# An AdaLN block on one core: batch 4's second FFN half behind the last projection, two of the last products and the sixth batch's shift on GpSimd

## The chip, the cores and the metric

The kernel runs on one NeuronCore of a Trainium2 chip. The metric is the device time in microseconds of one execution; three runs of the kernel before gave 286.42, 286.42 and 287.06 us, median 286.42. TensorE, VectorE, ScalarE and GpSimd run side by side, each through its own queue in order; SyncE issues all DMA. They meet only at semaphores.

## What is computed

Eight batches (B = 8) of 512 tokens by 256 channels, all fp32. Each goes through a layer norm modulated by rows made from a condition, an attention with 16 heads in which token i sees itself and i - 2^k (ten offsets, 0 to 256), a projection with gate and residual, a second modulated layer norm, a quantisation to fp6 in blocks of 32 (then scaled back), one 256x256 linear layer (called FFN), and gate and residual again.

```python
h = _layernorm(x) * (1 + ca) + sa
x = x + ga * attention(h, Wq, bq, Wk, bk, Wv, bv, Wo, bo)
h = _layernorm(x) * (1 + cb) + sb
xq, xs = _mx_quantize(h); wq, ws = _mx_quantize(weight)
x = x + gb * ((xq * xs) @ (wq * ws).T + bias)
```

The scores outside the ten offsets are 0, not minus infinity, so the softmax counts them: `out` is a sum of ten products of weights and shifted rows of v, plus a mean of v.

## The kernel before

Tokens lie on 128 partitions in four tiles (`NT` = 4), so a batch is a 128x1024 tile; a half is two tiles. The order of the work on each engine is written out by hand in five blocks (`block.sync`, `gpsimd`, `tensor`, `scalar`, `vector`), each a list of small functions; every function waits on counted semaphores and then issues. `LAST` is 7. Batches 0 to 5 are in a pipeline loop; the tail, after some 210 us, is written out call by call, and the change lies wholly there. In it:

- **Batch 7's products** (`pv_product(LAST, n)`, L1851). VectorE multiplies softmax weights (in the PSUM tile `ps45`) by the rows of v for ten offsets, n = 0 to 9. TensorE transposes each into `ps01` and sums it there (`last_product`, L919: eight matmuls for a product, six for n = 8, four for n = 9). ScalarE then seeds `ps45` with the residual (`seed_projection`, L1334), takes the sum out of `ps01` (`evacuate_last_attention`, L1352), and TensorE projects it (`project(LAST)`, L988).
- **Batch 6's second norm.** `project(LAST-1)`, then on ScalarE `take_x1`, `squares_after` (L1238, ending in the variance, L1242), on GpSimd `rstd_after` (L666, L668), on ScalarE `norm_after` (L1174); GpSimd scales by a modulation row (`scale_sixth`, L683) and VectorE adds the other (`shift_sixth`, L1766). VectorE then does `block_maxima`, `quantise`, `dequantise`.
- **Batch 7's second norm** is done in halves: VectorE's `last_variance` (L1595 to L1605) for half 0, GpSimd's `rstd_after(LAST, 0)`, ScalarE's `norm_last(0)` (L1174 with `v_shift`).
- **The gated FFN weights.** GpSimd multiplies `wT` by the row `row_gb` (`gate_ffn`, L639). There is one `row_gb` buffer: SyncE's `load_row_gb(b)` (L433) waits until gate b-1 is done, and gate b waits for the load.
- **Batch 4's FFN** (LAST-3) is in halves, both in `ps67`: `ffn(LAST-3, 1)` stands between the summed attention of batch 6 and `project(LAST-1)` on TensorE. `take_result` (L1407) copies a finished half out on ScalarE and counts `s_outb` ("out_ready").
- **Batch 5's FFN** (LAST-2) is in `ps23`, behind `xd_transposes(LAST-2)` (L1009), a copy of the transposes by ScalarE (`evacuate_xd`, L1365) and three filler matmuls (`keep_busy`, L752).

## Time and profile before

| | |
|---|---|
| median of 3 runs | 286.42 us |
| span of the profiled execution | 285.0 us |
| VectorE busy | 258.8 us (91%) |
| TensorE matmul busy | 255.6 us (90%) |
| ScalarE busy | 212.5 us (75%) |
| GpSimd busy | 210.5 us (74%) |
| granted TensorE clock, mean | 1.000 |

The span is from the first to the last instruction of one execution; the time of a run is 1.4 us longer than it. Busy shares are over the whole span; what counts for this change is which engine waits for which in the last 45 us, and that is in the timeline.

### The profile page before, as it was taken

The numbers are of one execution on the slowest core, as the hardware profiler recorded it, in microseconds if no ns is written. First come the engines' busy times: TensorE is split into PE (matmuls) and PEld (weight loads), VectorE is DVE, ScalarE is ACT, GpSimd is POOL, SyncE is SP. The second block draws the span as 40 slices with busy tenths as digits, with TensorE's granted clock in tenths as the row PEclk, the third lists the DMA queues.
The fourth block names the chain that finished last, engine by engine and source line by source line (L and its number), as shares of the span: only waits on it lengthen the run. The fifth ranks groups of instructions, "written<-read, shape, count | busy, mean of one in ns | idle before, by whom it ended". The sixth has DMA issues, their size and how long they took to land.

```text
span 285.0 us, 4442 instructions
## 1 busy us (share of the span) xinstructions
PE 255.6 (90%) x1368; PEld 158.8 (56%) x1368; DVE 258.8 (91%) x326; ACT 212.5 (75%) x577; POOL 210.5 (74%) x152
## 2 busy tenths in 40 slices
PE   6999997697978795989999999999999988997885
PEld 1653554175526561666556646664567646794663
DVE  3699799969995999999999999999999999999970
ACT  2386987975697779879898989887776937575752
POOL 7101439895879999999999999999999699845100
PEclk9999999999999999999999999999999999999999
DMA  7743977694784239724993389347943965730005
GB/s 225 193 181 81 340 248 232 230 338 133 240 273 148 73 125 350 251 72 131 295 336 127 129 263 286 135 113 222 333 147 94 279 198 178 230 103 11 0 26 199
DMA packets 54399, 53.91 MB, mean 189 GB/s; under 512 B 4100, under 2 KB 52824, under 8 KB 54376
## 3 DMA queue, kind: packets, MB, share of 16 engines
q1 hardware_dynamic: 54376, 53.63, 60.1%
q8 instruction: 11, 0.18, 0.3%
q14 instruction: 12, 0.10, 0.1%
HBM read 44.90 MB, written 8.72 MB: 188 GB/s over the span
## 4 chain that ended last, share of the span: by engine, by line
DVE 39%; POOL 19%; PE 18%; issue 11%; ACT 11%; DVEq 0%; POOLq 0%; ACTq 0%
POOL pv_buf L677 14%; DVE prod L1721 9%; DVE pv_buf L1851 9%; DVE prod L1851 4%; DVE prod L1710 4%; PE ps L988 3%; PE ps L1067 3%; PE ps L826 2%; ACT dump L1197 2%; PE ps L853 2%; ACT dump L1238 1%; DVE ps L1825 1%; PE ps L837 1%; DVE ps L1827 1%; POOL rstd L658 1%
## 5 line engine op out<-in xcount | busy, mean ns | idle before, releaser
L677 POOL TENSOR_TENSOR pv_buf<-pv_buf 128x1024 f32<-128x1024 f32 (+2 forms) x60 | 132.5, 2209 | 15.0 <-DVE pv_buf L1851 9.8
L1721 DVE TENSOR_TENSOR prod<-ps,kT 128x1024 f32<-128x1024 f32 (+4 forms) x70 | 75.1, 1110 | 0.0
L1851 DVE TENSOR_TENSOR pv_buf<-v_shift,ps 128x1024 f32<-128x1024 f32 x49 | 59.1, 1212 | 0.0
L937 PE MATMUL ps<-prod,sel_sum 128*32 128x512 f32 x256 | 30.8, 598 | 8.5 <-DVE prod L1721 7.8
L853 PE MATMUL ps<-wT,h_cen 128*128 128x256 f32 x128 | 29.9, 379 | 0.0
L826 PE MATMUL ps<-hT,wT 128*128 128x512 f32 x64 | 29.7, 596 | 0.0
L837 PE MATMUL ps<-hT,wT 128*128 128x512 f32 x64 | 29.3, 599 | 0.0
L988 PE MATMUL ps<-wo_g,w_raw 128*128 128x256 f32 x112 | 27.9, 392 | 0.0
L853 PEld LDWEIGHTS ps<-wT,h_cen 128*128 128x128 f32 x128 | 23.9, 190 | 6.4 <-issue 3.8
L988 PEld LDWEIGHTS ps<-wo_g,w_raw 128*128 128x128 f32 x112 | 20.1, 189 | 5.4 <-issue 3.2
L937 PEld LDWEIGHTS ps<-prod,sel_sum 128*32 128x32 f32 x256 | 6.7, 109 | 28.0 <-issue 13.8
L1067 PE MATMUL ps<-wf_g,w_raw 128*128 128x256 f32 x80 | 19.7, 391 | 0.0
L1851 DVE TENSOR_TENSOR pv_buf<-v_base,ps 128x1024 f32<-128x1024 f32 (+2 forms) x21 | 19.4, 950 | 0.2
L1291 ACT ACTIVATE kT<-ps,bias_cols 128x512 f32<-128x512 f32 x16 | 10.9, 686 | 11.6 <-PE ps L826 11.6
L649 POOL TENSOR_TENSOR rstd<-var,minus_half 128x4 f32<-128x4 f32 x4 | 4.1, 1016 | 20.1 <-ACT var L1201 19.3
L1174 ACT ACTIVATE x_norm<-x_in,shift,rstd 128x256 f32<-128x256 f32 x28 | 14.5, 594 | 5.6 <-POOL shift L651 3.2
L837 PEld LDWEIGHTS ps<-hT,wT 128*128 128x128 f32 x64 | 11.7, 190 | 12.4 <-issue 12.4
L826 PEld LDWEIGHTS ps<-hT,wT 128*128 128x128 f32 x64 | 11.6, 190 | 10.5 <-issue 9.0
L1067 PEld LDWEIGHTS ps<-wf_g,w_raw 128*128 128x128 f32 x80 | 14.5, 189 | 3.6 <-issue 2.0
L1174 ACT ACTIVATE x_norm<-x,shift,rstd 128x256 f32<-128x256 f32 x28 | 14.5, 592 | 1.4 <-POOL shift L668 1.4
L380 POOL TENSOR_TENSOR h<-x_norm,rows_mod 128x1024 f32<-128x1024 f32 x6 | 14.2, 2362 | 0.5
L375 POOL TENSOR_TENSOR x_norm<-x_norm,rows_mod 128x1024 f32<-128x1024 f32 x6 | 14.2, 2364 | 0.3 <-ACT x_norm L1174 0.2
(212 smaller groups left out, 550.3 us busy)
## 6 DMA issues: line engine op xcount, KB each, us to landing
v_shift<-v_rows SPq DMA_DIRECT2D x56, 512.0 KB, 5.7
x_in<-in_L_attn_x SPq DMA_DIRECT2D x8, 512.0 KB, 4.4
v_rows<-v_base SPq DMA_DIRECT2D x8, 512.0 KB, 4.1
x_res<-in_L_attn_x SPq DMA_DIRECT2D x8, 512.0 KB, 6.5
out_x<-outb SPq DMA_DIRECT2D x5, 512.0 KB, 5.8
rows_mod<-mod_rows SPq DMA_DIRECT2D x7, 256.0 KB, 3.4
x<-in_L_wmod SPq DMA_DIRECT2D x1, 1024.0 KB, 7.9
row_ga<-mod_rows SPq DMA_DIRECT2D x8, 128.0 KB, 4.9
```

The lines of the kernel that those rows point to most:

```text
L375: ops.tensor_tensor(normed[:, t, :], normed[:, t, :], rows[:, 0:1, :].broadcast_to([P, n, D]), ALU.mult).then_inc(scaled, 1)
L380: ops.tensor_tensor(dst[:, t, :], normed[:, t, :], rows[:, 1:2, :].broadcast_to([P, n, D]), ALU.add).then_inc(done, 1)
L677: nc.gpsimd.tensor_tensor(dst, dst, ring(b, n)[:, t:NT, :], ALU.add).then_inc(s_add, 1)
L826: mm = nc.tensor.matmul(ps23[:, j, :], wT[:, 1, k, P * j:P * j + P], hT[:, k, :], start=(k == 1), stop=(k == 0))
L837: mm = nc.tensor.matmul(ps01[:, j, :], wT[:, 0, k, P * j:P * j + P], hT[:, k, :], start=False, stop=(k == NC - 1), skip_group_check=True)
L853: mm = nc.tensor.matmul(ps23[:, k2, col:col + D], h_cen[:, k, P * t:P * t + P], wT[:, 2, k, :], start=(t % 2 == 0 and k == 0), stop=(t % 2 ...
L937: mm = nc.tensor.matmul(ps23[32 * g:32 * g + 32, 1, :], sel_sum[:, which, c, :], prod[:, n, c, :], start=(c == 0 and which == 0), stop=(c ...
L988: mm = nc.tensor.matmul(ps[:, k2, col:col + D], attnT[:, k, P * t:P * t + P], wo_by[b][:, k, :], start=False, stop=(t % 2 == 1 and k == NC ...
L1067: mm = nc.tensor.matmul(ps[:, half_, col:col + D], xdT_by[b][:, k, P * t:P * t + P], wf_by[b][:, k, :], start=False, stop=(t % 2 == 1 and ...
L1174: ins = nc.scalar.activation(dst[:, t, :], src[:, t, :], ACT.Identity, scale=rstd[:, t:t + 1], bias=shift[:, t:t + 1])
L1721: nc.vector.tensor_tensor(prod[:, n, :, o:L], ps01[:, :, o:L], kT[:, b % 2, :, 0:L - o], ALU.mult).then_inc(s_prod, 1)
L1851: nc.vector.tensor_tensor(dst[:, t:NT, :].rearrange("p t (h e) -> p t h e", e=DH), v_n.rearrange("p t (h e) -> p t h e", e=DH), weights, A ...
```

## The change

GpSimd takes over three pieces: batch 7's products 8 and 9 (new `far_product`, with their weights normalised first into the SBUF tile `w_far`), and the shift of batch 6, so that it does the whole `modulate`. Its queue is reordered around them. TensorE sums the products in the order 0, 1, 8, 2, 9, 3 to 7. `ffn(LAST-3, 1)` moves behind `project(LAST)` and `xd_transposes(LAST-2)`, into the second bank of `ps23`, which `open_late_ffn` opens with one matmul; the filler matmuls go. As `ffn(LAST-2, 0)` writes that bank too, it now waits for `s_outb` to reach 10, that is for `take_result(LAST-3, 1)`, and this stands on ScalarE behind `squares_after(LAST, 1)`. SyncE's loads are reordered, with the store of batch 4 behind them.

```diff
             engine.wait_ge(scaled, n_scaled)
+            if b == LAST - 1:
+                engine.wait_ge(s_prod, NO * B)
...
             load_x_res(LAST)
             load_rows_mod(LAST - 1)
-            load_row_gb(LAST - 1)
             load_bias_att(LAST)
             load_rows_last()
+            load_row_gb(LAST - 1)
             load_row_gb(LAST)
+            load_bias_ffn(LAST - 1)
+            store(LAST - 3)
             load_bias_ffn(LAST)
...
+            def far_product(n):
+                t = tiles_of(n)
+                i = POOL_LAST.index(n)
+                if i == 0:
+                    pool.wait_ge(s_wfar, 1)
+                    pool.wait_ge(s_v, NC * B)
+                    pool.wait_ge(s_sp, 2 * B)
+                nc.gpsimd.tensor_tensor(
+                    last_out(n)[:, t:NT, :].rearrange("p t (h e) -> p t h e", e=DH),
+                    v_base[:, LAST % 2, 0:NT - t, :].rearrange("p t (h e) -> p t h e", e=DH),
+                    w_far[:, t:NT, i, :].unsqueeze(3).broadcast_to([P, NT - t, HEADS, DH]),
+                    ALU.mult).then_inc(s_far, 1)
...
             modulate(pool, nc.gpsimd, LAST - 2)
-            gate_ffn(LAST - 2)
+            for n in POOL_LAST:
+                far_product(n)
             gate_projection(LAST)
             rstd_after(LAST - 1)
+            gate_ffn(LAST - 2)
+            modulate(pool, nc.gpsimd, LAST - 1)
             gate_ffn(LAST - 1)
-            scale_sixth()
             gate_ffn(LAST)
             rstd_after(LAST, 0)
...
+            def open_late_ffn():
+                pe.wait_ge(s_d, B)
+                nc.tensor.matmul(ps23[:, 1, :], ones3[0:NSPLIT, 0:P], ones3[0:NSPLIT, :], start=True, stop=True,
+                                 skip_group_check=True).then_inc(s_fopen, 1)
...
                     if b == LAST - 2:
                         pe.wait_ge(s_d, B)
+                        pe.wait_ge(s_outb, 2 * (LAST - 2))
...
             summed_attention()
-            ffn(LAST - 3, 1)
+            open_late_ffn()
             project(LAST - 1)
-            for n in range(NO):
+            for n in (0, 1, 8, 2, 9, 3, 4, 5, 6, 7):
                 last_product(n)
             project(LAST)
             xd_transposes(LAST - 2)
-            keep_busy(ps23, 0, 3)
+            ffn(LAST - 3, 1)
             ffn(LAST - 2, 0)
...
                 if b == LAST:
-                    act.wait_ge(s_pv, NO * B)
-                else:
-                    act.wait_ge(s_outb, 2 * (LAST - 3) + k2 + 1)
+                    act.wait_ge(s_pv, NO * LAST + NDVE_LAST)
+                else:
+                    act.wait_ge(s_outb, 2 * (LAST - 3) + 1 - k2)
...
             evacuate_summed()
-            take_result(LAST - 3, 1)
             seed_projection(LAST - 1, 1)
+            seed_ffn_half(LAST - 3, 1)
...
             squares_after(LAST, 1)
+            take_result(LAST - 3, 1)
             quantised(LAST - 1)
...
+                if b == LAST:
+                    first = SLOT[POOL_LAST[0]]
+                    nc.vector.tensor_tensor(w_far[:, :, :, :], w[:, :, first:, :], per_head(z_inv, NS - first),
+                                            ALU.mult).then_inc(s_wfar, 1)
+                    nc.vector.tensor_tensor(w[:, :, 0:first, :], w[:, :, 0:first, :], per_head(z_inv, first),
+                                            ALU.mult).then_inc(s_w, 1)
...
-            for n in range(NO):
+            for n in range(NDVE_LAST):
                 pv_product(LAST, n)
             block_maxima(LAST - 2)
             quantise(LAST - 2)
-            shift_sixth()
             last_variance()
```

GpSimd's queue in the tail, before: from batch 5's shift (L380) to the first reciprocal root of batch 7 (L666 with 128x2). `row_gb` rows are FFN gates, `row_ga` rows the projection's.

```order
L380 TENSOR_TENSOR h2<-x1_norm,rows_mod 128x1024 [waits zq_ready,x1_norm_scaled]
L639 TENSOR_TENSOR wf_g<-wT,row_gb 128x512 [waits ffn_in_psum,ffn_gate_loaded]
L626 TENSOR_TENSOR wT<-wT,row_ga 128x512 [waits v_mean_in_psum,v_in_psum,attention_gate_loaded]
L666 TENSOR_TENSOR rstd<-var,minus_half 128x4 [waits layer_norm2_variance_ready]
L668 TENSOR_TENSOR shift<-negmean,rstd 128x4 [waits layer_norm2_pool_step]
L639 TENSOR_TENSOR wT<-wT,row_gb 128x512 [waits q_in_psum,ffn_gate_loaded]
L683 TENSOR_TENSOR x1_norm<-x1_norm,rows_mod 128x1024 [waits x1_norm_ready,modulation_rows_loaded]
L639 TENSOR_TENSOR wT<-wT,row_gb 128x512 [waits q_in_psum,ffn_gate_loaded]
L666 TENSOR_TENSOR rstd<-var,minus_half 128x2 [waits layer_norm2_variance_ready]
L668 TENSOR_TENSOR shift<-negmean,rstd 128x2 [waits layer_norm2_pool_step]
```

And in the changed kernel (L695 are the two far products, L382 and L389 scale and shift, L675 and L677 root and shift factor, L648 the FFN gates):

```order
L389 TENSOR_TENSOR h2<-x1_norm,rows_mod 128x1024 [waits zq_ready,x1_norm_scaled]
L695 TENSOR_TENSOR prod<-v_base,w_far 128x768 [waits scores_in_psum,v_ready,last_far_weights_ready]
L695 TENSOR_TENSOR prod<-v_base,w_far 128x512
L635 TENSOR_TENSOR wT<-wT,row_ga 128x512 [waits v_mean_in_psum,v_in_psum,attention_gate_loaded]
L675 TENSOR_TENSOR rstd<-var,minus_half 128x4 [waits layer_norm2_variance_ready]
L677 TENSOR_TENSOR shift<-negmean,rstd 128x4 [waits layer_norm2_pool_step]
L648 TENSOR_TENSOR wf_g<-wT,row_gb 128x512 [waits ffn_in_psum,ffn_gate_loaded]
L382 TENSOR_TENSOR x1_norm<-x1_norm,rows_mod 128x1024 [waits x1_norm_ready,modulation_rows_loaded]
L389 TENSOR_TENSOR kT<-x1_norm,rows_mod 128x1024 [waits qk_products_ready,x1_norm_scaled]
L648 TENSOR_TENSOR wT<-wT,row_gb 128x512 [waits q_in_psum,ffn_gate_loaded] x2
L675 TENSOR_TENSOR rstd<-var,minus_half 128x2 [waits layer_norm2_variance_ready]
L677 TENSOR_TENSOR shift<-negmean,rstd 128x2 [waits layer_norm2_pool_step]
```

The gate of batch 5 (`wf_g`) has gone behind batch 6's root, batch 6's shift (`kT`) has joined its scale, and the last two gates, which had the scale between them, now stand one right behind the other, ahead of batch 7's root.

TensorE's queue, before: from the transposes of batch 5's quantised rows (L1009) to its FFN.

```order
L1009 MATMUL ps0<-ident,zq 128x128 [waits attention_ready,xd_ready]
L1009 MATMUL ps0<-ident,zq 128x128 x7
L752 MATMUL ps1<-ones3 128x512 x3
L1037 MATMUL ps1<-bias_ffn,ones3 128x512 [waits scores_less_max,ffn_bias_loaded_1,xdT_ready]
L1037 MATMUL ps1<-bias_ffn,ones3 128x512
L1067 MATMUL ps1<-wf_g,w_raw 128x256 [waits wf_gated]
L1067 MATMUL ps1<-wf_g,w_raw 128x256 x3
```

And in the changed kernel:

```order
L1034 MATMUL ps0<-ident,zq 128x128 [waits attention_ready,xd_ready]
L1034 MATMUL ps0<-ident,zq 128x128 x7
L1062 MATMUL ps1<-bias_ffn,ones3 128x512 [waits x1_in_ffn_banks,ffn_bias_loaded_0,xdT_ready]
L1093 MATMUL ps1<-w_raw,hT 128x256 [waits wf_gated]
L1093 MATMUL ps1<-w_raw,hT 128x256 x3
L1062 MATMUL ps1<-bias_ffn,ones3 128x512 [waits scores_less_max,out_ready,ffn_bias_loaded_1,xdT_ready]
L1062 MATMUL ps1<-bias_ffn,ones3 128x512
L1093 MATMUL ps1<-wf_g,w_raw 128x256 [waits wf_gated]
L1093 MATMUL ps1<-wf_g,w_raw 128x256 x3
```

The filler matmuls on `ps1` have given way to the bias (first L1062) and four matmuls (first L1093, two rows) of batch 4's second half, and the first matmul of batch 5's FFN (ps1, second L1062) has the new wait out_ready.

ScalarE's queue, before: from the copy of those transposes (L1365) to the second half's norm.

```order
L1365 ACTIVATE w_raw<-ps0 128x512 [waits ffn_in_psum,xdT_in_psum]
L1365 ACTIVATE w_raw<-ps0 128x512
L1234 ACTIVATE negmean<-sum2 128x2 [waits layer_norm2_pool_step,x1_ready]
L1238 ACTIVATE dump,sq2<-ps2,negmean 128x256 [waits layer_norm2_act_step]
L1238 ACTIVATE dump,sq2<-ps2,negmean 128x256
L1242 ACTIVATE var<-sq2 128x2 [waits layer_norm2_act_step]
L1421 ACTIVATE q8<-zq,tie 128x1024 [waits xd_ready,zq_ready,constants_made]
L1174 ACTIVATE v_shift<-ps2,shift,rstd 128x256 [waits layer_norm2_pool_step]
```

And in the changed kernel:

```order
L1391 ACTIVATE w_raw<-ps0 128x512 [waits ffn_in_psum,xdT_in_psum]
L1391 ACTIVATE w_raw<-ps0 128x512
L1260 ACTIVATE negmean<-sum2 128x2 [waits layer_norm2_pool_step,x1_ready]
L1264 ACTIVATE dump,sq2<-ps2,negmean 128x256 [waits layer_norm2_act_step]
L1264 ACTIVATE dump,sq2<-ps2,negmean 128x256
L1268 ACTIVATE var<-sq2 128x2 [waits layer_norm2_act_step]
L1436 ACTIVATE x_in<-ps1 128x512 [waits ffn_in_psum]
L1450 ACTIVATE q8<-zq,tie 128x1024 [waits xd_ready,zq_ready,constants_made]
L1200 ACTIVATE v_shift<-ps2,shift,rstd 128x256 [waits layer_norm2_pool_step]
```

The row `x_in<-ps1` is `take_result(LAST-3, 1)`, which counts out_ready; it stands behind batch 7's variance.

## Rows read from the trace of the kernel before

**Rows 1.** Chain of waits, 180 to 286 us: start, length, engine, tile, line

```profile
244.92 10.60 DVE prod L1851 x10
...
258.45 2.22 DVE kT L1766
...
272.40 0.39 PE ps L1037 x2
```

**Rows 2.** Timeline, TensorE: start, length, line, tiles, shapes, count, idle before

```profile
244.35 0.38 PE L978 MATMUL ps<-bias_att,ones 3*128 3x512 bf16 x1
...
248.74 8.24 PE L919 MATMUL ps<-ident,prod 128*128 128x128 f32 x74
...
258.05 1.97 PE L988 MATMUL ps<-wT,w_raw 128*128 128x256 f32 x8 [0.75 <-ACT w_raw L1352]
...
265.67 0.39 PE L1037 MATMUL ps<-bias_ffn,ones 3*128 3x512 bf16 x2 [0.43 <-ACT w_raw L1365]
...
265.99 3.72 PE L1067 MATMUL ps<-wf_g,w_raw 128*128 128x256 f32 x16
...
270.01 1.09 PE L1009 MATMUL ps<-ident,zq 128*128 128x128 f32 x8 [0.31 <-DVE zq L1778]
```

**Rows 3.** Timeline, ScalarE, same columns

```profile
242.31 1.25 ACT L1343 ACTIVATE w_raw<-ps,v_mean 128x512 f32<-128x512 f32 x2
...
253.78 2.08 ACT L1174 ACTIVATE x_norm<-x,shift,rstd 128x256 f32<-128x256 f32 x4 [1.41 <-POOL shift L668]
...
257.07 1.57 ACT L1352 ACTIVATE w_raw<-ps,v_mean 128x256 f32<-128x256 f32 x4 [0.20 <-issue]
...
263.30 1.02 ACT L1174 ACTIVATE v_shift<-ps,shift,rstd 128x256 f32<-128x256 f32 x2 [0.16 <-POOL shift L668]
...
264.53 1.09 ACT L1365 ACTIVATE w_raw<-ps 128x512 f32<-128x512 f32 x2 [0.21 <-PE ps L1009]
...
266.79 0.20 ACT L1242 ACTIVATE var<-sq 128x2 f32<-128x2 f32 x1
```

**Rows 4.** Timeline, GpSimd, same columns

```profile
243.37 2.36 POOL L380 TENSOR_TENSOR h<-x_norm,rows_mod 128x1024 f32<-128x1024 f32 x1
...
252.44 1.02 POOL L666 TENSOR_TENSOR rstd<-var,minus_half 128x4 f32<-128x4 f32 x1 [4.26 <-ACT var L1242]
...
258.32 1.27 POOL L639 TENSOR_TENSOR wT<-wT,row_gb 128x512 f32<-128x512 f32 x1
...
262.29 0.70 POOL L666 TENSOR_TENSOR rstd<-var,minus_half 128x2 f32<-128x2 f32 x1 [2.71 <-DVE var L1605]
...
267.07 1.15 POOL L666 TENSOR_TENSOR rstd<-var,minus_half 128x2 f32<-128x2 f32 x1 [3.81 <-ACT var L1242]
```

**Rows 5.** GpSimd's instructions grouped by line and shape: busy us, mean ns

```profile
L677 POOL TENSOR_TENSOR pv_buf<-pv_buf 128x768 f32<-128x768 f32 x6 | 10.9, 1818 | 0.9
```

**Rows 6.** Timeline, SyncE; and row_gb's eight loads, issue to landing

```profile
255.01 0.32 SPq L433 DMA_DIRECT2D row_gb<-mod_rows  x1
...
DMA to landing us min/median/max: 2.9/3.9/4.8
```

**Rows 7.** Timeline, VectorE, same columns

```profile
260.59 0.75 DVE L1595 BATCH_NORM_STATS2 stats<-ps 128x6 f32<-128x256 f32 x2
...
262.13 1.21 DVE L1778 TENSOR_TENSOR zq<-q,ps 128x1024 f32<-128x1024 fp8e4 x1
...
265.11 1.23 DVE L1750 TENSOR_TENSOR zq<-kT,tail_inv 128x1024 f32<-128x1024 f32 x1
```

**Rows 8.** Timeline, TensorE, span's end and start; a window, clock behind POOL

```profile
280.77 1.03 PE L1067 MATMUL ps<-wT,h_cen 128*128 128x256 f32 x4
...
285.00:285.20 0.20, 0.00 (x0) 0.00 (x0) 0.00 (x0) 0.00 (x0) 0.00 (x0) 0.82 0.00 0
...
11.12 1.06 PE L782 MATMUL ps<-ident,w_raw 128*128 128x128 f32 x4
...
15.68 0.60 PE L782 MATMUL ps<-ident,w_raw 128*128 128x128 f32 x4
```

More of the change, by code:

```diff
@@ L56, in adaln_block @@
     PE_SUMMED = [7, 8, 9]
+    POOL_LAST = [8, 9]
+    NDVE_LAST = NO - len(POOL_LAST)
     GA, GB, CB, SB = range(4)
@@ L146, in adaln_block @@
         em = sb("em", [P, NT, HEADS])
+        w_far = sb("w_far", [P, NT, len(POOL_LAST), HEADS])
         z_inv = sb("z_inv", [P, NT, HEADS])
@@ L251, in adaln_block @@
         s_lacc = sem("pv_last_product_taken")
+        s_wfar = sem("last_far_weights_ready")
+        s_far = sem("last_far_product_done")
+        s_fopen = sem("late_ffn_bank_opened")
         s_vmp = sem("v_mean_in_psum")
@@ L299, in adaln_block @@
         TAIL = LAST - 3
+        LATE_FFN = (LAST - 3, 1)
         PAIRED = (LAST - 2, LAST - 1)
@@ L552, in _ @@
             shift_v(LAST, 7)
-            store(LAST - 3)
-            load_bias_ffn(LAST - 1)
             load_x_res(LAST)
             load_rows_mod(LAST - 1)
-            load_row_gb(LAST - 1)
             load_bias_att(LAST)
             load_rows_last()
+            load_row_gb(LAST - 1)
             load_row_gb(LAST)
+            load_bias_ffn(LAST - 1)
+            store(LAST - 3)
             load_bias_ffn(LAST)
@@ L913, in last_product @@
             def last_product(n):
-                pe.wait_ge(s_pv, NO * LAST + n + 1)
+                if n in POOL_LAST:
+                    pe.wait_ge(s_far, POOL_LAST.index(n) + 1)
+                else:
+                    pe.wait_ge(s_pv, NO * LAST + n + 1)
                 if n == 0:
@@ L919, in last_product @@
                         mm = nc.tensor.matmul(ps01[:, c, P * t:P * t + P], last_out(n)[:, t, P * c:P * c + P],
-                                              ident[:, :], start=(n == 0 and t == 0), stop=(n == NO - 1),
+                                              ident[:, :], start=(n == 0 and t == 0), stop=(n == NDVE_LAST - 1),
                                               is_transpose=True, skip_group_check=True)
                 mm.then_inc(s_lacc, 1)
+            def open_late_ffn():
+                pe.wait_ge(s_d, B)
+                nc.tensor.matmul(ps23[:, 1, :], ones3[0:NSPLIT, 0:P], ones3[0:NSPLIT, :], start=True, stop=True,
+                                 skip_group_check=True).then_inc(s_fopen, 1)
             def head_sums(b, which):
@@ L1047, in ffn @@
                     pe.wait_ge(s_xdTl, half_ + 1)
-                ps = {LAST - 2: ps23, LAST: ps45}.get(b, ps67)
+                ps = ps23 if (b, half_) == LATE_FFN else {LAST - 2: ps23, LAST: ps45}.get(b, ps67)
                 pe.wait_ge(s_bffn[b % 2], 16 * (b // 2 + 1) + 16 * (b >= LAST - 2))
@@ L1384, in seed_ffn_half @@
                     act.wait_ge(*((s_x1, b + 3) if half_ else (s_x1h, 1)))
+                elif (b, half_) == LATE_FFN:
+                    act.wait_ge(s_fopen, 1)
                 else:
                     act.wait_ge(s_outb, 2 * b + half_ - 1)
-                nc.scalar.activation(ps67[:, half_, :].rearrange("p (t c) -> p t c", c=D),
+                ps = ps23 if (b, half_) == LATE_FFN else ps67
+                nc.scalar.activation(ps[:, half_, :].rearrange("p (t c) -> p t c", c=D),
                                      x1_of(b)[:, 2 * half_:2 * half_ + 2, :], ACT.Copy).then_inc(s_fseed, 1)
@@ L1405, in take_result @@
                     act.wait_ge(s_out, 16 * (LAST - 3))
-                ps = ps67 if b < LAST else ps45
+                ps = ps23 if (b, half_) == LATE_FFN else ps67 if b < LAST else ps45
                 nc.scalar.activation(out_by[b][:, 2 * half_:2 * half_ + 2, :],
@@ L1543, in _ @@
             evacuate_half_xd(0)
-            seed_ffn_half(LAST - 3, 1)
             evacuate_half_xd(1)
@@ L1760, in scale_to_psum @@
                 dve.wait_ge(s_scale, 1)
-            def shift_sixth():
-                b = LAST - 1
-                dve.wait_ge(s_mod, b + 1)
-                dve.wait_ge(s_prod, NO * B)
-                nc.vector.tensor_tensor(h2_by[b], x1_norm[:, :, :], rows_mod[:, 1:2, :].broadcast_to([P, NT, D]),
-                                        ALU.add).then_inc(s_h2, 1)
             def dequantise(b, half_=None):
@@ L1826, in softmax_weights @@
                 link(nc.vector.reciprocal(z_inv[:, :, :], z_sum))
-                nc.vector.tensor_tensor(w, w, per_head(z_inv, NS), ALU.mult).then_inc(s_w, 1)
+                if b == LAST:
[4 more added lines that the diff above has]
+                                            ALU.mult).then_inc(s_w, 1)
+                else:
+                    nc.vector.tensor_tensor(w, w, per_head(z_inv, NS), ALU.mult).then_inc(s_w, 1)
                 assert k[0] == NSM
```

6 lines of the change are left out of this document (removed).

## The prediction

> **What bounds the kernel now.** I read the chain of waits for the tail first, then each engine's timeline there. The chain puts ten products on VectorE from 244.92 to 255.52, VectorE's shift of batch 6 at 258.45, and from 272.40 to the end TensorE without a gap [rows 1]. The timelines correct it in one place. TensorE's 74 transposes of the products run from 248.74 for 8.24 us, to 256.98, one behind the other [rows 2]; ScalarE's copy of their sum starts at 257.07 [rows 3], 1.5 us after VectorE's last product. So TensorE, not VectorE, bounds that stretch. Behind it VectorE bounds: its variance of batch 7 starts at 260.59 [rows 7], when the shift is over (258.45 and 2.22), though the projection's half that it reads was done at 260.02 (258.05 and 1.97) [rows 2]. The last meeting is at 270.01: the transposes of batch 6's quantised rows wait 0.31 us for VectorE, and TensorE's own work before them ends at 269.71 (265.99 and 3.72) [rows 2]. TensorE has only those 0.3 us to spare. Whatever delays the start of these transposes delays the end by as much.
>
> **Part 1, batch 4's half out of the way.** The projection of batch 6 starts at 244.35 [rows 2], but what it needs, ScalarE's copy, is complete at 243.56 (242.31 and 1.25) [rows 3]. With a hand-over of 0.06 it starts at 243.62, 0.73 earlier. The opening matmul (0.4, like the bias row at 244.35) hides in the wait for that copy. All that hangs on it goes 0.73 earlier: the transposes of the products, the copy (256.34), the first half of the last projection (259.3), and batch 6's norm, which ends at 255.13 (253.78 and 2.08, less 0.73) [rows 3].
>
> **Part 2, products 8 and 9 on GpSimd.** VectorE is done 1.4 us earlier (two products between the last 1024-wide one and 255.52, less 0.07 for splitting the weights' normalisation), but TensorE's 74 transposes stay 74: nothing comes of it there. On GpSimd they cost 1.82 (768 wide) [rows 5] and 1.27 (512 wide, as the gate at 258.32) [rows 4]. They start when batch 5's shift ends at 245.73 (243.37 and 2.36); with the projection's gate GpSimd is free by 250.1, and batch 6's root is due at 251.7 (252.44 less 0.73) [rows 4]. Slack 1.6, cost nothing. The trace has no GpSimd product with a broadcast innermost operand; bounds are the same price and twice it (3.1 more, of which 1.5 shows).
>
> **Part 3, the shift on GpSimd.** Scale and shift follow the norm: 255.27, then 2.36, 0.09 and 2.36 [rows 4], to 260.08. Batch 6's gate comes next, to 261.3. VectorE needs the shift only after 262. So far it is covered, and VectorE could start the variance at 259.35, 1.24 earlier than before. But VectorE's shift at 258.45 took 2.22 [rows 1] where its equal-sized step with two SBUF operands at 265.11 took 1.23 [rows 7]; it began under GpSimd's gate (258.32 to 259.59) and ended 1.1 after it [rows 4]. I read this as waiting for GpSimd. The reverse shows too: the two-column root took 0.70 alone and 1.15 at 267.07 [rows 4]. By this the small steps of the variance, all SBUF with SBUF, due at 260.15 (0.8 into it), wait for the gate's end at 261.3. The dequantisation, 1.54 behind the start before (260.59 to 262.13) [rows 7], then comes at 262.04 and the variance at 262.1: as before, the gain is gone. The Trainium skill (SBUF — State Buffer, "Who interferes with whom") says the same, that a VectorE instruction with two SBUF inputs and a GpSimd one that reads SBUF exclude each other for the whole instruction; without it the variance would be ready at 261.0, and still wait for GpSimd, below.
>
> **Part 4, the gates in a row.** This decides. There is one `row_gb` buffer. Before, batch 7's row was issued at 255.01 [rows 6], when batch 6's gate was done, and its landing was hidden by the scale: batch 7's gate ran at 258.32 [rows 4]. Now batch 6's gate ends at 261.3, SyncE issues then, and GpSimd's next instruction waits for the landing, with batch 7's root queued behind it. Loads of this row took 2.9 to 4.8 us [rows 6]; the one at 255.01 at most 3.3, by the gate that used it, in a stretch as quiet as this. I take 2.9: the gate runs from 264.25 to 265.5. The root then starts at 265.5, or up to 1.2 later if VectorE's two-operand quantisation (2.98 behind the dequantisation, [rows 7], so due at 265.02 and held back by the gate) goes first. ScalarE's norm of batch 7 follows the start of the root by 1.01 (262.29 to 263.30) [rows 3, 4]: 266.5 to 267.7, middle 267.1. Before: 263.30.
>
> **Part 5, what stands behind that norm.** On ScalarE, in order: the norm (1.02), the copy of batch 5's transposes and batch 7's second variance (2.46, from 264.53 to 266.99) [rows 3], and now batch 4's result, 0.6 by a 512-wide copy. That makes 268.05, 270.45 and 271.0. Batch 5's FFN waits for exactly this result, since it overwrites the bank. It starts at 271.05 in place of 265.67 and takes 4.04 (265.67 to 269.71) [rows 2]: TensorE is free for batch 6's transposes at 275.1 instead of 270.01, 5.1 later. VectorE's rows for them are there by 273.4 (quantised copy and dequantisation behind 271.0). Before, ScalarE was 0.15 late for the copy that follows; now it is not. Net +4.95.
>
> **The rest, at nothing.** SyncE's loads for batch 7 are issued at 246 to 251 and used from 255 on. The store of batch 4 behind 271 has over 10 us. Batch 6's and 7's FFN biases (1.5 KB) are issued at about 266.6 and 275.1, some 6 us or more ahead of use. The new wait of the shift on the score products was met before 240.
>
> **Sum without the clock.** 285.0 of span and 4.95, with the 1.4 us between span and median run: 291.4.
>
> **The clock.** TensorE finishes batch 4's half at about 266.6 (transposes at 263.3, 1.09; then half of 4.04 and the hand-over) and stands idle to 271.05, 4.4 us. Nothing that long is in the tail of the trace, except the end: the last matmul ends at 281.80, and the granted clock is half of full, 1.2 instead of 2.4 GHz, from about 285.13 (mean 0.82 from 285.0 to 285.2), 3.3 us later [rows 8]. Four transposes at half rate took 1.06 (at 11.12), at full 0.60 (at 15.68) [rows 8]. By this batch 5's FFN would start at half rate; its 4.04 us lengthen by 0 to 4.04. I take 1.3, a third, since the stretch is dense and the clock should come back within it. The Trainium skill (TensorE: Matmul & The Clock Gate, "Why this matters for your kernels") warns of gaps between bursts of matmuls for this reason; it speaks against taking out the filler matmuls.
>
> **Rivals.** (a) The forecast: gates in a row, and the clock falls: 285.0 + 4.95 + 1.3 + 1.4 = 292.7. (b) The same without the fall, for example because the idle time is shorter than 4.4 or one fall at the end says little about when: 291.4, with 290.4 if the root goes ahead of VectorE and the landing is short, 292.2 the other way. (c) A slower landing (4.8) or GpSimd products at twice the price: 1.5 to 1.9 more on either, 293 to 295.4. (d) Not slower: GpSimd's root for batch 7 is not late. It decides at 262.7: if the norm of batch 7's first half starts by then, ScalarE's chain of 1.02, 2.46 and 0.6 ends by 266.8, the FFN by 270.9, and the end comes at most 0.9 later. At best, with the variance at 261.0 and the norm at 262.1, the FFN ends at 270.3, 0.3 later: 286.7. For it speaks that the early finish of parts 1 and 2 is real; against it, that the last gate's row cannot be issued before 261.3 by the order of the queues. (e) Faster: the variance 1.24 earlier and nothing else late, 285.2. Against it: TensorE's 0.3 us at 269.71, with 2.2 us of batch 4's work now in that stretch against 0.8 of filler.
>
> **How the numbers follow.** (a) 0.50, (b) 0.37, (c) 0.07, (d) 0.04, (e) 0.02. The time is that of (a), 292.7. The range runs from the low end of (b), 290.4, to the high end of the clock's price and (c), 295.4, and leaves out some 0.13. A difference under 0.3% (0.86 us) can't be told from none here: faster 0.02, same 0.04, slower 0.94.
>
> **What would show it.** In the changed kernel: the projection of batch 6 about 0.7 earlier; the 74 transposes as long as before; GpSimd idle for about 2.9 us between the last two gates; the norm of batch 7's first half on ScalarE near 267 instead of 263.3; TensorE idle for over 4 us ahead of batch 5's FFN, with the granted clock at 0.5 in part of the FFN. I am wrong if the last gate starts before 263, if the FFN of batch 5 starts before 269, or if the waits in between belong to another engine.

## The result, and the profile after

The changed kernel takes 294.74 us, median of four runs (294.07 to 295.57). The kernel before, run beside it, takes 286.74, also of four (286.42 to 289.52). The ratio is 1.026, with a 95% interval of 1.022 to 1.030: slower by 8.0 us. The profiled execution has a span of 293.3 us, against 285.0.

TensorE in the changed kernel, from its timeline (start, length, line, operation, tiles, shapes, count, idle time before it and what ended that); these rows answer to [rows 2]:

```profile
243.69 0.37 PE L1003 MATMUL ps<-bias_att,ones 3*128 3x512 bf16 x1 [1.14 <-ACT w_raw L1369]
...
248.06 8.24 PE L939 MATMUL ps<-ident,prod 128*128 128x128 f32 x74
...
264.56 1.99 PE L1093 MATMUL ps<-w_raw,hT 128*128 128x256 f32 x8
...
271.79 0.61 PE L1062 MATMUL ps<-bias_ffn,ones 3*128 3x512 bf16 x2 [5.24 <-ACT x_in L1436]
...
272.33 6.27 PE L1093 MATMUL ps<-wf_g,w_raw 128*128 128x256 f32 x16
...
278.44 1.04 PE L1034 MATMUL ps<-ident,zq 128*128 128x128 f32 x8
```

The projection of batch 6 and the 74 transposes come 0.7 us earlier, as the change wants. Then TensorE stands idle for 5.24 us ahead of batch 5's FFN, and that FFN takes 6.8 us (271.79 to 278.60) in place of 4.04. The transposes of batch 6's rows start 8.4 us later than before (278.44 for 270.01); behind them TensorE has no gap that matters, as before.

Why it waits stands in the timelines of GpSimd, ScalarE and VectorE (same columns). GpSimd's answer to [rows 4]:

```profile
245.30 2.51 POOL L695 TENSOR_TENSOR prod<-v_base,w_far 128x768 f32<-128x768 f32 x2
...
251.77 1.02 POOL L675 TENSOR_TENSOR rstd<-var,minus_half 128x4 f32<-128x4 f32 x1 [2.73 <-ACT var L1268]
...
257.76 2.35 POOL L389 TENSOR_TENSOR kT<-x_norm,rows_mod 128x1024 f32<-128x1024 f32 x1
...
260.07 1.27 POOL L648 TENSOR_TENSOR wT<-wT,row_gb 128x512 f32<-128x512 f32 x1
...
264.56 1.27 POOL L648 TENSOR_TENSOR wT<-wT,row_gb 128x512 f32<-128x512 f32 x1 [3.22 <-DMA row_gb<-mod_rows]
...
265.79 1.69 POOL L675 TENSOR_TENSOR rstd<-var,minus_half 128x2 f32<-128x2 f32 x1
```

ScalarE's, to [rows 3]:

```profile
256.39 1.57 ACT L1378 ACTIVATE w_raw<-ps,v_mean 128x256 f32<-128x256 f32 x4 [0.20 <-issue]
...
267.78 1.02 ACT L1200 ACTIVATE v_shift<-ps,shift,rstd 128x256 f32<-128x256 f32 x2 [5.32 <-POOL shift L677]
...
271.07 0.58 ACT L1436 ACTIVATE x_in<-ps 128x512 f32<-128x512 f32 x1
```

VectorE's, to [rows 7], with the first row of the tail:

```profile
240.34 0.89 DVE L1828 TENSOR_TENSOR score_buf<-ps,mx 128x320 f32<-128x320 f32 x2
...
259.38 0.76 DVE L1624 BATCH_NORM_STATS2 stats<-ps 128x6 f32<-128x256 f32 x2 [2.40 <-PE ps L1013]
...
260.18 1.18 DVE L1628 TENSOR_TENSOR mean<-stats 128x2 f32<-128x2 f32 x1
...
261.95 1.22 DVE L1800 TENSOR_TENSOR zq<-q,ps 128x1024 f32<-128x1024 fp8e4 x1
...
264.93 1.98 DVE L1779 TENSOR_TENSOR zq<-kT,tail_inv 128x1024 f32<-128x1024 f32 x1
```

Read downwards: batch 6's gate ends at 261.34; only then is the last row issued, it lands 3.1 us later, the last gate runs at 264.56, and batch 7's root stands behind it. The chain of waits over the last 54 us (start, length, engine, tile, line) goes through just these:

```profile
261.37 3.12 DMA row_gb<-mod_rows
...
264.56 1.27 POOL wT L648
...
265.83 1.66 POOL rstd L675
```

Windows of the changed kernel show the clock (stretch, its length, busy us with count of PE, PEld, DVE, ACT and POOL, granted clock, DMA share, GB/s):

```profile
270.50:271.00 0.50, 0.00 (x0) 0.00 (x0) 0.50 (x1) 0.47 (x3) 0.00 (x0) 0.69 0.00 0
...
274.00:276.00 2.00, 2.00 (x6) 1.55 (x6) 1.97 (x4) 0.72 (x1) 0.00 (x0) 0.50 0.08 25
...
277.50:278.00 0.50, 0.50 (x3) 0.41 (x3) 0.47 (x2) 0.00 (x0) 0.00 (x0) 0.98 0.00 0
```

It is at 2.4 GHz until about 270.7, then at 1.2, and back at about 277.5: nearly all of batch 5's FFN lies under it.

To compare kernels from one profile each I use the **tail**: from the start of VectorE's pair of `score_buf<-ps,mx` (240.34 above) to the span's end. It leaves out that the kernels reach this point at slightly different times (239.76 to 240.56). The kernel before has it here:

```profile
240.49 0.89 DVE L1806 TENSOR_TENSOR score_buf<-ps,mx 128x320 f32<-128x320 f32 x2
```

That makes 285.0 - 240.49 = 44.5 us before and 293.3 - 240.34 = 53.0 after. A tail comes from one execution, a median from 4 to 12, so a difference of some tenths between tails has to be seen in the medians too. Each ratio is to the kernel before as it ran beside that kernel (medians 286.74 to 286.83).

| kernel | median us | ratio to before, 95% | tail us | against before |
|---|---|---|---|---|
| before | 286.74 | | 44.5 | |
| after | 294.74 | 1.022 to 1.030 | 53.0 | +8.5 |
| e1_gate_behind | 287.72 | 0.999 to 1.006 | 45.8 | +1.3 |
| e2_filler | 294.54 | 1.018 to 1.030 | 52.5 | +8.0 |
| e3_second_row | 290.33 | 1.003 to 1.017 | 48.2 | +3.7 |
| e4_both_behind | 286.71 | 0.995 to 1.000 | 44.7 | +0.2 |
| e5_dense_filler | 295.54 | 1.022 to 1.033 | 53.4 | +8.9 |
| e8_five_dense_fillers | 292.38 | 1.012 to 1.024 | 49.9 | +5.4 |
| p1_products_only | 286.61 | 0.995 to 1.001 | 44.7 | +0.2 |
| p2_shift_only | 287.89 | 1.000 to 1.006 | 45.0 | +0.5 |
| p3_late_ffn_only | 287.28 | 0.997 to 1.003 | 45.3 | +0.8 |
| e6_gates_apart_late_bias | 286.57 | 0.994 to 1.000 | 44.2 | -0.3 |
| e7_split_ffn | 286.02 | 0.992 to 0.998 | 44.0 | -0.5 |
| e9_split_behind | 285.91 | 0.993 to 0.998 | 43.6 | -0.9 |

### The profile page after: what moved, and what is told of

Its sections match the earlier page's. It is cut to its first block, busy times and chain, and to the rows that moved or that the text cites. A ratio compares the mean times of both kernels' runs of the same rounds, so it can differ in the third digit from the quotient of the medians.

```text
span 293.3 us, 4441 instructions
## 1 busy us (share of the span) xinstructions
PE 258.8 (88%) x1366; PEld 161.2 (55%) x1366; DVE 257.3 (88%) x324; ACT 212.1 (72%) x577; POOL 215.9 (74%) x155
## 4 chain that ended last, share of the span: by engine, by line
PE 46%; POOL 19%; ACT 12%; DVE 12%; issue 8%; DMA 2%; POOLq 0%; DVEq 0%; ACTq 0%
POOL pv_buf L686 13%; PE ps L1093 8%; PE ps L1013 7%; PE ps L870 4%; PE ps L854 4%; PE ps L843 4%; DVE prod L1739 3%; PE ps L962 3%; DVE prod L1750 3%; DVE pv_buf L1880 2%; PE ps L939 2%; ACT dump L1223 2%; ACT dump L1264 2%; PE ps L897 2%; POOL x_norm L382 2%
## 5 line engine op out<-in xcount | busy, mean ns | idle before, releaser
L1013 PE MATMUL ps<-wo_g,w_raw 128*128 128x256 f32 x112 | 29.3, 406 | 0.0
L1013 PEld LDWEIGHTS ps<-wo_g,w_raw 128*128 128x128 f32 x112 | 20.9, 197 | 5.8 <-issue 3.4
L1093 PE MATMUL ps<-wf_g,w_raw 128*128 128x256 f32 x80 | 22.2, 429 | 0.0
L1093 PEld LDWEIGHTS ps<-wf_g,w_raw 128*128 128x128 f32 x80 | 16.3, 213 | 4.6 <-issue 2.2
L382 POOL TENSOR_TENSOR x_norm<-x_norm,rows_mod 128x1024 f32<-128x1024 f32 x7 | 16.5, 2361 | 1.3 <-ACT x_norm L1200 1.2
L1243 ACT ACTIVATE x<-ps 128x256 f32<-128x256 f32 x28 | 10.4, 380 | 7.1 <-PE ps L1013 7.1
```

The lines of the kernel that those rows point to most:

```text
L382: ops.tensor_tensor(normed[:, t, :], normed[:, t, :], rows[:, 0:1, :].broadcast_to([P, n, D]), ALU.mult).then_inc(scaled, 1)
L1013: mm = nc.tensor.matmul(ps[:, k2, col:col + D], attnT[:, k, P * t:P * t + P], wo_by[b][:, k, :], start=False, stop=(t % 2 == 1 and k == NC ...
L1093: mm = nc.tensor.matmul(ps[:, half_, col:col + D], xdT_by[b][:, k, P * t:P * t + P], wf_by[b][:, k, :], start=False, stop=(t % 2 == 1 and ...
```

## The experiments

**The theory** is that of the prediction: the two last gates in a row, with one row buffer, delay batch 7's root; batch 5's FFN, which now waits for a result behind that root, is late; TensorE's clock falls in the idle time. The rivals are that the late half itself, the shift or the products cost the time, or that the FFN is slow for another reason than the clock.

**Is it the order of the gates?** The last gate goes behind the first root of batch 7; all else stays.

```
             gate_ffn(LAST - 1)
-            gate_ffn(LAST)
             rstd_after(LAST, 0)
+            gate_ffn(LAST)
             rstd_after(LAST, 1)
```

> The changed kernel with one line moved: GpSimd's last FFN gate (batch 7) stands behind batch 7's first root instead of ahead of it. Theory (the root is held up by the landing of the gate's row): the root starts when VectorE's variance is there, about 262.05 instead of 265.79; the norm of batch 7's first half starts at about 263.05 instead of 267.78; batch 4's result ends at 267.4 and batch 5's FFN starts at about 267.5 instead of 271.79, with TensorE idle under 1 us ahead of it and the clock at full. Its 4.05 us end at 271.55, 1.5 after the 270.01 of the kernel before: span 286.5, some 288. Rival (the new wait of batch 5's FFN for batch 4's result, or the added work on TensorE, is the cause, and the gate only fills idle time): the FFN starts at 270 or later and the span stays over 290.

Measured: 287.72 us, a tail of 45.8, 7.2 us shorter than the changed kernel's. GpSimd and TensorE in its timeline:

```profile
261.66 0.71 POOL L675 TENSOR_TENSOR rstd<-var,minus_half 128x2 f32<-128x2 f32 x1 [0.77 <-DVE var L1634]
...
263.85 1.27 POOL L648 TENSOR_TENSOR wT<-wT,row_gb 128x512 f32<-128x512 f32 x1 [1.21 <-DMA row_gb<-mod_rows]
...
266.99 0.39 PE L1062 MATMUL ps<-bias_ffn,ones 3*128 3x512 bf16 x2 [0.89 <-ACT x_in L1436]
```

The root comes at 261.66 and not at 265.79. The last gate still waits for its row, but nobody waits for it. The FFN starts 4.8 us earlier (4.4 counted from the tail's start), at full clock. One call in another place takes back 7.2 of the 8.5 us; 1.3 are left.

**Is it the landing?** Batch 7's row gets a buffer of its own (`row_gb_last`), so that its load waits for no gate; the queue of GpSimd is unchanged. The wait of the load, with the lines that choose the buffer left out:

```
...
-                if b > 0:
+                if b == LAST:
+                    sp.wait_ge(s_rowgb, 16 * b)
+                elif b > 0:
                     sp.wait_ge(s_wfg, b)
...
```

> The changed kernel with a buffer of its own for batch 7's FFN gate row, loaded once batch 6's row has landed; GpSimd's order is untouched, both gates still ahead of the root. Theory (the landing, not GpSimd's work, is what costs): the last gate follows the one before at 261.3, the root starts at about 262.6, the norm at 263.6, batch 5's FFN at 267.8: span 286.8. Rival (GpSimd simply has too much to do ahead of the root): the root starts after 264 and the span is 289 or more.

Measured: 290.33 us, with the four executions spread from 288.87 to 292.17. The profiled one has a span of 288.4, 1.6 more than the 286.8 that I expected. The two gates follow each other at once, and VectorE's variance stands against both:

```profile
259.89 1.15 DVE L1633 TENSOR_TENSOR mean<-stats 128x2 f32<-128x2 f32 x1
...
260.98 1.26 POOL L653 TENSOR_TENSOR wT<-wT,row_gb_last 128x512 f32<-128x512 f32 x1
...
261.04 1.23 DVE L1635 TENSOR_TENSOR var<-stats 128x2 f32<-128x2 f32 x1
...
263.98 1.76 PE L1039 MATMUL ps<-ident,zq 128*128 128x128 f32 x8 [2.68 <-DVE zq L1805]
...
269.68 0.39 PE L1067 MATMUL ps<-bias_ffn,ones 3*128 3x512 bf16 x2 [0.78 <-ACT x_in L1441]
```

and the clock falls in spite of the short wait (windows of this kernel):

```profile
264.00:264.50 0.50, 0.50 (x4) 0.50 (x5) 0.50 (x1) 0.50 (x2) 0.00 (x0) 0.74 0.00 0
...
267.50:268.00 0.50, 0.50 (x3) 0.39 (x3) 0.47 (x2) 0.50 (x3) 0.00 (x0) 0.85 0.00 0
```

I had missed both. With the gates back to back, two small steps of the variance, not one, last as long as a gate. That delays VectorE's dequantisation and with it batch 5's transposes; TensorE is idle for 2.68 us, and the clock falls at 264.24, when the transposes have already begun. It stays at 1.2 GHz for some 3.4 us. So taking the landing away alone buys 4.8 of the 8.5 us in this execution; the gates' place costs something without it. How much of the rest is the clock is open: another of the four executions had a span of 287.1, and the last section shows that the clock can fall or not behind one and the same wait.

**And with no gate ahead of either root?** GpSimd's order becomes root of half 0, gate 6, root of half 1, gate 7.

```
-            gate_ffn(LAST - 1)
-            gate_ffn(LAST)
             rstd_after(LAST, 0)
+            gate_ffn(LAST - 1)
             rstd_after(LAST, 1)
+            gate_ffn(LAST)
```

> The changed kernel with both last gates behind the roots (root of batch 7's first half, gate 6, second root, gate 7). Theory (GpSimd's gate of batch 6 also holds up the small two-operand steps of VectorE's variance): the first of them takes 0.16 instead of 1.18 us, the variance is there at 261.0 instead of 262.03, the norm starts at 262.0, the FFN of batch 5 at about 266.4 and ends at 270.45: span 285.5, 1.0 less than with the last gate alone moved. Rival (no exclusion between the two engines; the 1.18 has another reason): the variance is there at 262.0 as before and the span is that of the kernel with one gate moved, about 286.5.

Measured: 286.71 us. VectorE's first small step and GpSimd's root:

```profile
259.90 0.17 DVE L1628 TENSOR_TENSOR mean<-stats 128x2 f32<-128x2 f32 x1
...
260.82 0.71 POOL L675 TENSOR_TENSOR rstd<-var,minus_half 128x2 f32<-128x2 f32 x1 [0.98 <-DVE var L1634]
```

0.17 us instead of 1.18: with no GpSimd instruction beside it the step is a seventh. The root is 0.8 earlier than in e1 (1.0 counted from the tail's start), and the transposes of batch 6 come at 270.02, as before the change. The tail is 1.1 us shorter than e1's, which is about what this one step had lost (1.0). VectorE's dequantisation of batch 6 (L1800 at 267.32) now lies beside gate 7 and takes 2.01 us, but it ends at 269.33, when TensorE is still at batch 5's FFN (to 270.19), and so costs nothing there.

**Each part alone.** Three kernels are the one before with one part of the change each, every one with the gates where they stood before (gate, scale, gate, root, or gate, scale and shift, gate, root). The diffs are the matching pieces of the change's diff: the products and their order on TensorE; the shift on GpSimd; batch 4's half, its bank and wait, and the loads.

> The kernel before with one part alone: products 8 and 9 on GpSimd, with their order on TensorE. Theory (TensorE's 74 transposes bound that stretch, and the shift waits for GpSimd's scale behind it): VectorE is done with its products 1.4 us earlier and then waits for the scale; span as before, 285.0, within 0.2. Rival (VectorE's load counts): span 284 or less.

> The kernel before with one part alone: batch 6's shift on GpSimd behind its scale, products and FFN as before. Theory (GpSimd's gate of batch 7 at 260.8 to 262.0 holds up the small two-operand steps of VectorE's variance): the first of them takes over 1 us, the variance comes at about 262.9 instead of 262.2, batch 6's transposes at 270.5: span 285.6, 0.5 over the kernel before. Rival (taking 2.2 us off VectorE pays): the variance starts at 260.1 and is ready at 261.7, span 284.8 or less.

> The kernel before with one part of the change alone: batch 4's second FFN half behind the last projection in the other bank, with its loads, seeds and result moved as in the change. Products and shift stay on VectorE, the gates keep their old order with the scale between the last two. Theory (this part gives 0.7 early and costs about 1.8 late, through the wait of batch 5's FFN for the result, but no stall of 4 us and no fall of the clock): batch 6's projection starts 0.7 earlier, batch 5's FFN starts at 267.0, span 286.1. Rival (this part carries the loss): the FFN starts at 270 or later, span over 289.

Measured: tails +0.2, +0.5 and +0.8, medians 286.61, 287.89 and 287.28. Their intervals all reach 1.000. The profiled execution of the shift alone was among its fastest (287.07; the median is 1.1 us over the kernel before), so its +0.5 is a low figure. With the products alone VectorE is done early and then waits 1.47 us for GpSimd's scale; with the shift alone batch 6's gate stands beside the variance, as predicted:

```profile
260.71 1.18 DVE L1601 TENSOR_TENSOR mean<-stats 128x2 f32<-128x2 f32 x1
```

With the late half alone the new wait shows, 0.89 us for batch 4's result, but the root ahead of that result is not late:

```profile
267.03 0.39 PE L1044 MATMUL ps<-bias_ffn,ones 3*128 3x512 bf16 x2 [0.89 <-ACT x_in L1418]
```

Alone they make 1.4 together by the unrounded tails, and 1.5 by the medians; the whole change makes 8.5 and 8.0. The rest is in none of the three but, as e1 shows, in GpSimd's order: with gate 6 moved behind the shift, nothing is left between the two gates that could hide the landing. Batch 5's gate behind batch 6's root and the new order of the loads were not run alone.

**Is the slow FFN the clock, and would fillers hold it?** Three kernels put matmuls whose results nobody uses between batch 4's half and batch 5's FFN: 20 short ones with three rows of weights (the `keep_busy` that the change took out), then dense ones with 128 rows, 128x512 fp32.

```
             ffn(LAST - 3, 1)
+            keep_busy(ps23, 0, 20)
             ffn(LAST - 2, 0)
```

> The changed kernel with 20 filler matmuls (512 columns, 0.21 us each, some 4.3 us) in TensorE's idle stretch ahead of batch 5's FFN. Nothing else moves. Theory (the clock falls in the idle stretch and the FFN pays for it): the granted clock stays 1.00, the FFN still starts at about 271.8 but takes 4.05 instead of 6.8 us, span 290.6, some 2.7 less. Rival (the FFN is slow from something else, or the fall is a matter of the whole stretch's load): the FFN stays over 6 us and the span at 293.

Measured: 294.54 us, nothing gained. TensorE's timeline and a window:

```profile
265.93 5.20 PE L769 MATMUL ps<-ones 3*128 3x512 bf16 x20
...
271.49 6.12 PE L1093 MATMUL ps<-wf_g,w_raw 128*128 128x256 f32 x16
...
269.50:270.00 0.50, 0.50 (x3) 0.15 (x1) 0.50 (x1) 0.47 (x3) 0.00 (x0) 0.56 0.00 0
```

TensorE was busy from 265.93 on and the clock fell all the same, at about 269.6. The spans of all four executions, 292.3 to 293.2, fit this. So the expectation was wrong in its assumption that any filler holds the clock, and said nothing yet on what the clock costs.

```
             ffn(LAST - 3, 1)
+            for _ in range(10):
+                nc.tensor.matmul(ps23[:, 0, :], ident[:, :], hT[:, 0, :], start=True, stop=True)
             ffn(LAST - 2, 0)
```

> The changed kernel with ten fp32 filler matmuls of 128 rows and 512 columns (0.44 us each, 4.4 us) ahead of batch 5's FFN, in place of the 20 with three rows that did not keep the clock up. Theory (the clock fell there because matmuls with three rows of weights count for little; dense ones hold it): the granted clock stays 1.00, the FFN starts at about 271.8 and takes 4.05 us instead of 6.8, span 290.6. Rival (the clock falls for another reason than TensorE standing idle or nearly so): it falls in spite of the dense filler and the span stays above 292.

Measured: 295.54 us, a failure in size: each of the ten ran as two, 20 of 0.44 us, 8.75 us in all, and pushed the FFN itself back. But the clock was at full throughout the tail, and the 16 matmuls of the FFN took 3.72 us. So five of them:

> The changed kernel with half as many dense filler matmuls as in the run before with dense ones (there each of 512 fp32 columns ran as two of 0.44 us, 8.7 us in all, and held up the FFN). Now 4.4 us, which fit in the idle stretch. Theory: the clock stays 1.00, batch 5's FFN starts at 271.8 as in the changed kernel and takes 4.05, span 290.5. Rival: the clock falls again, FFN 6.8 us, span 293.3.

Measured: 292.38 us, a tail of 49.9.

```profile
266.04 4.45 PE L1179 MATMUL ps<-hT,ident 128*128 128x512 f32 x10
...
271.25 0.39 PE L1062 MATMUL ps<-bias_ffn,ones 3*128 3x512 bf16 x2 [0.76 <-ACT x_in L1438]
...
271.57 3.72 PE L1093 MATMUL ps<-wf_g,w_raw 128*128 128x256 f32 x16
...
272.00:274.00 2.00, 2.00 (x11) 1.77 (x10) 1.82 (x3) 1.06 (x3) 0.00 (x0) 1.00 0.79 262
```

This separates the two causes. The FFN starts as late as in the changed kernel (0.2 us earlier once the drift ahead of the tail, 0.33, is taken off) and is as short as before. The tail is 3.1 us shorter than after's: 2.8 of it is the clock. The late start is the other 5.4. By the medians the fillers give back 2.4 (294.74 to 292.38), so the clock's price is 2.4 to 2.8.

**A version that keeps the gain.** What is good in the change is the 0.7 us of part 1. To keep it: gate 5 back ahead of batch 6's root, gate 6 behind that root and ahead of scale and shift (which hide the landing), gate 7 between the two roots of batch 7; and batch 5's FFN takes the second bank only for its second half, so that its first half waits for nothing.

```
             gate_projection(LAST)
-            rstd_after(LAST - 1)
             gate_ffn(LAST - 2)
-            modulate(pool, nc.gpsimd, LAST - 1)
+            rstd_after(LAST - 1)
             gate_ffn(LAST - 1)
-            gate_ffn(LAST)
+            modulate(pool, nc.gpsimd, LAST - 1)
             rstd_after(LAST, 0)
+            gate_ffn(LAST)
...
                     if b == LAST - 2:
                         pe.wait_ge(s_d, B)
-                        pe.wait_ge(s_outb, 2 * (LAST - 2))
...
+                elif b == LAST - 2:
+                    pe.wait_ge(s_outb, 2 * (LAST - 2))
                     bias_into(ps, 1, b, ROWS2)
```

> A version meant to keep the gains of the change. GpSimd: batch 5's gate ahead of batch 6's root, batch 6's gate right behind that root, batch 7's gate right behind batch 7's first root, so no two gates stand in a row and none under the variance. TensorE: the second bank's bias of batch 5's FFN, and its wait for batch 4's result, only ahead of its second half. Theory: the variance is undisturbed as with both gates behind (0.17 for its first small step), the FFN starts at 265.2 as soon as batch 4's half is over and ends at 269.3, batch 6's transposes start at 269.3 instead of 270.0 in the run with both gates behind: span 284.1, some 0.9 us under the kernel before. Rival (VectorE's chain binds behind the variance, whatever TensorE does): span 284.8 as with both gates behind.

Measured: 286.57 us, 8 us under the changed kernel and level with the one before (0.994 to 1.000); I had expected 0.9 less than before.

```profile
259.75 0.20 DVE L1631 TENSOR_TENSOR mean<-stats 128x2 f32<-128x2 f32 x1
...
269.47 1.04 PE L1034 MATMUL ps<-ident,zq 128*128 128x128 f32 x8
```

The variance has 0.20 instead of 1.18 for its first step, and batch 6's transposes start at 269.47. What bounds now is TensorE itself, without a gap from batch 5's transposes (261.81) to batch 6's: the half of batch 4 (bias 0.38 and matmuls 1.99) stands in that stretch whole. So the half is split by its tiles, tile 0 ahead of the last projection, where TensorE waits for ScalarE's copy, tile 1 behind it (the new third argument of `ffn` picks the tile):

```
+            ffn(LAST - 3, 1, 0)
             project(LAST)
+            ffn(LAST - 3, 1, 1)
             xd_transposes(LAST - 2)
-            ffn(LAST - 3, 1)
```

> As the run before in this call, and batch 4's late half is cut by tiles: its bias and first tile (1.3 us) stand ahead of the last projection, in the 1.0 us in which TensorE waits there for ScalarE's copy, its second tile (1.0 us) right behind the projection, in the wait for batch 5's transposes. Theory (TensorE's work between the projection and batch 6's transposes is the bound): the transposes of batch 6 start at 268.4, when VectorE's rows are there, span 283.2, 1.8 under the kernel before. Rival (ScalarE's chain of norm, copy, variance, result and quantised copy is the bound, and splitting TensorE's work only opens gaps): no gain on the run before, or a loss of 0.3 from the projection's later start.

Measured: 286.02 us, a span of 284.1 where I expected 283.2. The gap ahead of the projection is 0.75 us before [rows 2], a tile's share is about 1.4 (half of 1.99 and a bias row of 0.38), and so the projection started at 257.69 in place of e6's 256.94. The variance went with it. Better is tile 0 right behind the projection and tile 1 behind batch 5's transposes; then each lies in a wait of TensorE for another engine:

```
             project(LAST)
+            ffn(LAST - 3, 1, 0)
             xd_transposes(LAST - 2)
-            ffn(LAST - 3, 1)
+            ffn(LAST - 3, 1, 1)
```

> As the version with batch 4's late half cut by tiles, but nothing ahead of the last projection (there its start moved from 256.94 to 257.69 and with it the variance, 0.8 later): bias and first tile stand right behind the projection, the second tile behind batch 5's transposes, in TensorE's wait for ScalarE's copy of them. Theory: the variance is back at 259.75, the transposes of batch 5 run from 262.4 (0.6 later than with the half uncut), FFN from 264.7 to 268.9, the transposes of batch 6 start at 268.9 instead of 269.2 and 269.5: span 283.7. Rival (ScalarE, with its copies and squares in a row from 262 to 267, decides): no gain, 284.1.

Measured: 285.91 us, ratio 0.993 to 0.998: the lowest median, 8.8 us under the changed kernel and 0.8 under the one before; e7's interval (0.992 to 0.998) overlaps it, so the two are not told apart. The span is 284.2 where I expected 283.7. In its timeline TensorE is again the last to come ahead of batch 6's transposes: it has no gap there, and VectorE's rows are ready at 269.16, 0.3 us before:

```profile
261.55 0.38 PE L1062 MATMUL ps<-bias_ffn,ones 3*128 3x512 bf16 x1
...
267.60 1.99 PE L1097 MATMUL ps<-wf_g,w_raw 128*128 128x256 f32 x8
...
267.93 1.23 DVE L1806 TENSOR_TENSOR zq<-q,tail_scale 128x1024 f32<-128x1024 fp8e4 x1 [0.17 <-ACT q L1456]
...
269.43 1.04 PE L1034 MATMUL ps<-ident,zq 128*128 128x128 f32 x8
```

## Why the prediction was right, step by step

- **Parts 1 and 2 held.** Projection of batch 6: 243.62 predicted, 243.69 measured; copy of the sum 256.34 and 256.39; norm of batch 6 done at 255.13 and 255.19. The far products took 2.51 for both and not 3.09, and GpSimd still had 2.73 us of idle time ahead of batch 6's root; they were cheaper than even the lower bound of their price. VectorE's early finish was worth nothing (p1: +0.2).
- **Part 3 held**, the exclusion too: variance at 259.35 predicted, 259.38 measured; its small step took 1.18; the dequantisation came at 261.95 for 262.04. The Trainium skill (SBUF — State Buffer, "Who interferes with whom") has a VectorE instruction with two SBUF inputs contend with a GpSimd one that reads SBUF. The trace agrees, with its 1.18 beside the gate, and e4 gives the other side, 0.17 us with GpSimd idle.
- **Part 4 held, 0.7 us short.** The last gate ran at 264.56 and not at 264.25, because the row took 3.1 us to land and not the 2.9 that I took. Then VectorE's two-operand quantisation, issued in the same stretch, came first: it took 1.98 us instead of 1.23 and the root 1.69 instead of 0.70. So the norm came at 267.78, at the upper end that I gave (267.7), not at the middle (267.1). In e2 and e5, with the same queues on both engines, the root went first (0.71 us), so the order can come out either way.
- **Part 5 held, with a slip that did no harm.** From the norm's start to the result's end I had 3.9 us (267.1 to 271.0); the three steps that I named add up to 4.1. It took 3.87 (267.78 to 271.65). The FFN started at 271.79 for 271.05, the 0.7 of part 4 carried on.
- **The clock held as a mechanism, not in size.** I took 1.3 us of an open span from 0 to 4.04; it was 2.8 in the profile. A third was a guess. The fall came 4.1 us after the last matmul (266.55 to 270.69; 3.3 at the end of the span before, [rows 8]), just ahead of the FFN, and the assumption that a dense FFN would bring the clock back within a third of itself was wrong: it came back when the FFN was nearly over.

The sum: 4.95 + 0.7 of part 4 + 2.8 = 8.45, less 0.15 behind batch 6's transposes and in rounding, makes the 8.3 by which the span grew. Predicted were 4.95 + 1.3 = 6.25. Of the missing 2.05, 1.5 is the clock and 0.7 the order of root and quantisation and the landing, less that 0.15. Both errors went the same way, so the 294.74 came to lie near the top of the range, and it is the open price of the clock that made the range reach so far: (c) by its own terms ends at 292.7 + 1.9 = 294.6, not at 295.4.

Of the rivals, (b) fell with the clock in the windows above, (c) with the landing of 3.1 us and the products' 2.51, (e) with the root at 265.79. (d) is what e1 and e4 made by another order of the queue: once the root is at 261.7 or 260.8, the mechanism that I priced is gone. The bound that I gave for it was a norm by 262.7 and at most 0.9 more. Counted from the tail's start and put on the times of the kernel before, e4's norm came at 262.49, within the bound, with a tail of +0.2; e1's at 263.26, outside it, with +1.3.

Several expectations behind the prediction were off: e3 (a span of 286.8 for 288.4) missed the second gate beside the variance and the fall of the clock; e2 took any filler to hold the clock; e5 mis-sized it; e6, e7 and e9 hoped for 0.2, 0.9 and 0.5 us more than came.

## What to carry to other kernels

When work is moved off a queue, write down what the moved piece had been hiding: here the scale between two gates hid the landing of a row that one buffer allowed only after the first gate. An instruction that waits for a DMA should stand behind the ones that others wait for, even if it is ready first on paper. And a wait of some microseconds on TensorE has a second price, the clock, which is paid in the matmuls behind it: look at the granted clock there before adding up the parts.
